# Two normalisations of a step answered by one GpSimd addition and one power over eight columns

## The reference, cut to what matters

```python
def _layer_norm(t, gamma, beta):
    mu = jnp.mean(t, axis=-1, keepdims=True)
    var = jnp.mean(jnp.square(t - mu), axis=-1, keepdims=True)
    return (t - mu) * jax.lax.rsqrt(var + LN_EPS) * gamma + beta
...
moe_out = jnp.einsum('bseh,bse->bsh', expert_out, sparse)
return _layer_norm(x + moe_out, gamma, beta)
```

## Time and profile before

| | |
|---|---|
| median of three executions | 2806.18 us (2802.29 to 2806.91) |
| the profiled execution, its own time | 2819.77 us |
| span of its profile | 2817.9 us |
| busy: PE, DVE, ACT, POOL | 84%, 70%, 54%, 35% of the span |
| the phase that is changed | from about 1868 to 2325 us of the span |

### The profile page before, as it was taken

How to read it: one execution, slowest core, us unless ns; L and a number is a source line. 1 busy time by engine, 2 the same in 40 slices (tenths; PEclk the granted TensorE clock), 3 DMA queues, 4 the chain that set the end, 5 groups by cost and what they waited for, 6 DMA issues and landing times. The chain is left out here.

```text
span 2817.9 us, 45185 instructions
## 1 busy us (share of the span) xinstructions
PE 2376.4 (84%) x14046; PEld 1704.3 (60%) x14047; DVE 1983.6 (70%) x5404; ACT 1514.0 (54%) x2636; POOL 999.0 (35%) x1024
## 2 busy tenths in 40 slices
PE   8999999999996999999964999926788885666665
PEld 4444444444444788888854999925677774444443
DVE  6777777777745788888853444447687877888886
ACT  2444444444442667676743665636565651777776
POOL 1100100100000355555552444468776720344343
PEclk9999999999997999999976999967687786677676
DMA  2000000000002011111116777731111100000000
GB/s 56 0 18 13 0 18 13 0 9 1 0 1 86 27 45 48 47 47 47 47 58 204 256 255 256 253 98 51 46 46 41 47 13 22 20 24 22 25 25 25
DMA packets 69334, 162.68 MB, mean 58 GB/s; under 512 B 13009, under 2 KB 32662, under 8 KB 68894
## 3 DMA queue, kind: packets, MB, share of 16 engines
q1 hardware_dynamic: 39618, 94.16, 10.2%
q0 software_dynamic: 21504, 44.99, 5.5%
q10 hardware_dynamic: 8064, 21.68, 2.5%
HBM read 63.87 MB, written 63.88 MB: 45 GB/s over the span
## 5 line engine op out<-in xcount | busy, mean ns | idle before, releaser
L418 DVE TENSOR_REDUCE pmax<-ppre 112x1 f32<-112x512 f32 x656 | 424.0, 686 | 161.6 <-PE ppre L260 161.5
L211 ACT ACTIVATE prob<-pscore 128x896 f32<-128x896 f32 x336 | 308.1, 917 | 421.9 <-PE pscore L293 421.9
L307 PE MATMUL pout<-prob,xkey 128*64 128x448 f32 x1344 | 327.5, 566 | 0.4 <-ACT prob L211 0.4
L718 POOL DMA_INDIRECT rows_in<-xr,idx x224 | 233.9, 1044 | 237.2 <-DVE idx L1189 180.2
L260 PE MATMUL ppre<-xh,yh 49*112 49x512 f32 x656 | 291.1, 446 | 7.8 <-DVE pmax L418 4.2
L260 PEld LDWEIGHTS ppre<-xh,yh 49*112 49x112 f32 x656 | 112.6, 172 | 239.1 <-issue 104.2
L1631 POOL DMA_INDIRECT yg<-rows_out,place x224 | 234.7, 1048 | 62.4 <-issue 62.1
L193 POOL CAST yh<-ynext 113x448 fp32r<-113x448 f32 x28 | 17.3, 616 | 666.4 <-DVE pmax L418 638.4
L293 PE MATMUL pscore<-yh,xh 49*128 49x448 f32 x700 | 241.1, 422 | 0.4 <-DVE yh L438 0.4
L2146 POOL TENSOR_TENSOR yg<-y,gout 112x512 f32<-112x512 f32 x112 | 141.2, 1271 | 265.5 <-DVE y L2379 265.5
L1481 POOL TENSOR_TENSOR zl<-z,zh 128x448 fp32r<-128x448 f32 x126 | 144.7, 1149 | 219.2 <-ACT zh L1447 209.8
(11 more groups left out here) (367 smaller groups left out, 6464.5 us busy)
## 6 DMA issues: line engine op xcount, KB each, us to landing
wd<-down SPq DMA_DIRECT2D x63, 512.0 KB, 3.0
xb<-rows_in SPq DMA_DIRECT2D x63, 448.0 KB, 3.6
rows_out<-yb ACTq DMA_DIRECT2D x63, 336.0 KB, 3.2
out<-ho SPq DMA_DIRECT2D x28, 336.0 KB, 2.8
rows_in<-zero SPq DMA_DIRECT2D x15, 448.0 KB, 5.3
rows_in<-xr,idx POOLq DMA_INDIRECT x224, 2.5
yg<-rows_out,place POOLq DMA_INDIRECT x224
xkey<-in_xkey SPq DMA_DIRECT2D x4, 800.0 KB, 6.8
```

The lines of the kernel that those rows point to most:

```text
L211: nc.scalar.activation(prob[j % 3][:, :, :], pscore[j % 2][:, :, 0:CH], ACT.Exp).then_inc(exped, 1)
L307: mm = pe.matmul(pout[i * LO:(i + 1) * LO, 0:CH], xkey[b % 2][:, 2 * j + i, :], prob[j % 3][:, i, :], start=(j == 0), stop=(i == 1 and j = ...
L418: nc.vector.reduce_max(pmax[:, q, 2 * block + half:2 * block + half + 1], bank(u, depth), AX.X).then_inc(pre_max, 1)
L718: nc.gpsimd.indirect_dma_start(rows_in, bass.IndirectOffsetOnAxis(ap=idx[r % G3][:, 2 * q + k:2 * q + k + 1], axis=0), xr[r % G3][:, q, :] ...
```

## The change

The statistics of both normalisations go into one tile `agg3[T, 2, TPC, 2]`, and `veps3`, `rst3`, `eps5_3` and `mhalf_3` get the same extra index of 2. GpSimd's `factor(s+3)` and `factor4(s+2)` become one `factors(s+3)`. It waits for the aggregates of both, then does one addition and one power over [112, 8]. It stands where `factor` stood, ahead of the last two gathers of the step. `offset` reads column 0 of it, `offset4` column 1, and `offset4(g)` now waits for the same count as `offset(g+1)`.

```diff
-            def factor(g):
-                pool.wait_ge(S["agg_out"], g + 1)
-                nc.gpsimd.tensor_tensor(veps[:], agg[:, :, 1], eps5[:], ALU.add).then_inc(S["veps_out"], 1)
+            def factors(g):
+                cols = slice(0 if here(g) else 1, 2 if here(g - 1) else 1)
+                if here(g):
+                    pool.wait_ge(S["agg_out"], g + 1)
+                if here(g - 1):
+                    pool.wait_ge(S["agg4_out"], g)
+                nc.gpsimd.tensor_tensor(veps[:, cols, :], agg[:, cols, :, 1], eps5[:, cols, :],
+                                        ALU.add).then_inc(S["veps_out"], 1)
                 pool.wait_ge(S["veps_out"], g + 1)
                 if g >= 1:
                     pool.wait_ge(S["nrm_out"], g)
-                nc.gpsimd.tensor_tensor(rst[:], veps[:], mhalf[:], ALU.pow).then_inc(S["rst_out"], 1)
-
-            def factor4(g):
-
-                pool.wait_ge(S["agg4_out"], g + 1)
-                nc.gpsimd.tensor_tensor(veps4[:], agg4[:, :, 1], eps5[:], ALU.add).then_inc(S["veps4_out"], 1)
-                pool.wait_ge(S["veps4_out"], g + 1)
-                if g >= 1:
-                    pool.wait_ge(S["xn_ready"], g)
-                nc.gpsimd.tensor_tensor(rst4[:], veps4[:], mhalf[:], ALU.pow).then_inc(S["rst4_out"], 1)
+                if g >= 2:
+                    pool.wait_ge(S["xn_ready"], g - 1)
+                nc.gpsimd.tensor_tensor(rst[:, cols, :], veps[:, cols, :], mhalf[:, cols, :],
+                                        ALU.pow).then_inc(S["rst_out"], 1)

             for s in range(-LEAD, NC):
                 if here(s + 4):
                     gather_rows(s + 4, (0, 1, 2))
-                if here(s + 3):
-                    factor(s + 3)
+                if here(s + 3) or here(s + 2):
+                    factors(s + 3)
                 if here(s + 4):
                     gather_rows(s + 4, (3,))
-                if here(s + 2):
-                    factor4(s + 2)
...
             def offset4(g):
-                dve.wait_ge(S["rst4_out"], g + 1)
-                nc.vector.scalar_tensor_tensor(off4[:], agg4[:, :, 0], -1.0, rst4[:], ALU.mult,
+                dve.wait_ge(S["rst_out"], g + 2)
+                nc.vector.scalar_tensor_tensor(off4[:], agg[:, 1, :, 0], -1.0, rst[:, 1, :], ALU.mult,
                                                ALU.mult).then_inc(S["off4_out"], 1)
```

More of the change, by code:

```diff
@@ L1553, in linear_attention_phase @@
         bet = sb("bet3", [T, D])
-        eps5 = sb("eps5_3", [T, TPC])
-        mhalf = sb("mhalf_3", [T, TPC])
+        eps5 = sb("eps5_3", [T, 2, TPC])
+        mhalf = sb("mhalf_3", [T, 2, TPC])
         yg = [sb(f"yg3_{i}", [T, TPC, 2, D]) for i in range(2)]
@@ L1559, in linear_attention_phase @@
         bn = sb("bn3", [T, TPC, 6])
-        agg = sb("agg3", [T, TPC, 2])
-        veps = sb("veps3", [T, TPC])
-        rst = sb("rst3", [T, TPC])
+        agg = sb("agg3", [T, 2, TPC, 2])
+        veps = sb("veps3", [T, 2, TPC])
+        rst = sb("rst3", [T, 2, TPC])
         off = sb("off3", [T, TPC])
         bn4 = sb("bn4", [T, TPC, 6])
-        agg4 = sb("agg4", [T, TPC, 2])
-        veps4 = sb("veps4", [T, TPC])
-        rst4 = sb("rst4", [T, TPC])
         off4 = sb("off4", [T, TPC])
@@ L1595, in linear_attention_phase @@
         names = ("e_in", "w_in", "w_ready", "xa_out", "half_out", "acc_out", "stat_out", "agg_out", "veps_out",
-                 "rst_out", "off_out", "nrm_out", "dvec3", "hm_out", "stat4_out", "agg4_out", "veps4_out", "rst4_out",
+                 "rst_out", "off_out", "nrm_out", "dvec3", "hm_out", "stat4_out", "agg4_out",
                  "off4_out", "xn_ready", "xtr_mm", "xH_out", "xL_out", "xT_out", "qk_mm", "b_sum", "a_sum",
@@ L1822, in rows_normed @@
                     ac = nc.scalar.activation(yf[:, q, :], acc[g % 3][:, q, :], ACT.Identity, bias=off[:, q:q + 1],
-                                              scale=rst[:, q:q + 1])
+                                              scale=rst[:, 0, q:q + 1])
                 ac.then_inc(S["nrm_out"], 1)
@@ L1833, in normalise @@
                         ac = nc.scalar.activation(xn[g % 2][:, q, cols], h[:, t, src], ACT.Identity,
-                                                  bias=off4[:, q:q + 1], scale=rst4[:, q:q + 1])
+                                                  bias=off4[:, q:q + 1], scale=rst[:, 1, q:q + 1])
                 ac.then_inc(S["xn_ready"], 1)
@@ L1897, in add_experts @@
                 for q in range(TPC):
-                    ag = nc.vector.bn_aggr(agg[:, q, :], bn[:, q, :])
+                    ag = nc.vector.bn_aggr(agg[:, 0, q, :], bn[:, q, :])
                 ag.then_inc(S["agg_out"], 1)
@@ L1903, in offset @@
                 dve.wait_ge(S["rst_out"], g + 1)
-                nc.vector.scalar_tensor_tensor(off[:], agg[:, :, 0], -1.0, rst[:], ALU.mult,
+                nc.vector.scalar_tensor_tensor(off[:], agg[:, 0, :, 0], -1.0, rst[:, 0, :], ALU.mult,
                                                ALU.mult).then_inc(S["off_out"], 1)
@@ L1921, in add_moe @@
                 for q in range(TPC):
-                    ag = nc.vector.bn_aggr(agg4[:, q, :], bn4[:, q, :])
+                    ag = nc.vector.bn_aggr(agg[:, 1, q, :], bn4[:, q, :])
                 ag.then_inc(S["agg4_out"], 1)
             def offset4(g):
-                dve.wait_ge(S["rst4_out"], g + 1)
-                nc.vector.scalar_tensor_tensor(off4[:], agg4[:, :, 0], -1.0, rst4[:], ALU.mult,
+                dve.wait_ge(S["rst_out"], g + 2)
+                nc.vector.scalar_tensor_tensor(off4[:], agg[:, 1, :, 0], -1.0, rst[:, 1, :], ALU.mult,
                                                ALU.mult).then_inc(S["off4_out"], 1)
```

## The result

The changed kernel takes 2839.09 us (median of four executions, 2833.55 to 2841.30) beside 2804.23 us before: a ratio of 1.0118, interval 1.0103 to 1.0134, 35 us slower. The forecast was +24 us, 2830, with a range from 2809 to 2837: the first comparison lies above the range.

What follows compares the result with a forecast made beforehand. GpSimd and DVE were taken to set the pace together in steady steps. Late gathers gave 9.23 us, 17 x 0.83 made it 23.3, plus 2 less 0.4 to 2.7 at the turns: +24 us, 2830 us, range 2809 to 2837.

Steps and rivals of the forecast that it cites:

- T: End of the second normalisation's aggregates in a step, the last thing the second power needs; distances run from it to DVE's products.
- the loop closes: Late products delay the statistics queued behind them on DVE, hence the next T: a step of 14.26 us plus x.
- the second stretch: Four steady distances from T = 2056.37 to 2102.45: 19.92 us before, 22.16 forecast, +2.24 us and 4x.
- x: Extra time of a GpSimd power over eight columns against four: between 0 and 0.83 us, taken as 0.83.
- The first stretch: Eight steady distances from T = 1891.81 to the products at 1994.22: 41.37 us before, 44.32 forecast, +2.95 us and 8x.
- The three steps into a turn: Steps where gram_turned lies between T and products: the power's wait goes, -2.9 us in all; with x, -0.4 to -2.7.
- the turns: Six other distances at the turns: no change from gathers, but with x the second offset is late, +2 us in all.
- The phase: Time from the first T to the last, where the forecast's steps lie; 406.9 us in the first profile of before.
- rival 1: A power is paid for the instruction, not its columns: x near 0, +6 us, 2812; chance 0.25.
- rival 2: Faster: the late gathers land in time for DVE's products, -20 us, 2786; chance 0.08.
- rival 3: Gathers land later than forecast or the turns stretch, half a microsecond more a step: +33 us, 2839; chance 0.10.
- The rule on the landing: Gather data land 2.2 us from the issue's start, not 2.64: each distance 0.44 shorter, sum +16 us at x = 0.83.

Runs made afterwards that it cites:

- the place alone: The kernel before with the last two gathers of a step moved behind the second power, both additions and powers kept apart: 2817.7 against 2808.3 us, ratio 1.0033.
- the trial instructions: The changed kernel plus unused GpSimd additions and powers of 1 to 32 columns behind its last factors; whole time not used, power over 8 columns measured 1.64 us.
- the next two: The changed kernel, unchanged, compared again with the kernel before: 2833.5 against 2808.3 us, ratio 1.0090, then 2831.5 against 2805.3 us, ratio 1.0093.
- one late: The changed kernel with one gather behind the joined power instead of two: 2817.0 against 2805.3 us, ratio 1.0038.

## Why the prediction was right or wrong

**The sign and the mechanism were right**, step by step. GpSimd stands at its wait when T comes; the last two gathers start behind the power; the products wait for their landing in 21 steps (I gave 17 to 20); the loop closes through the statistics. Both halves are shown by doing them alone: the place alone gives distances of 5.5 us (forecast 5.54), the width in the trial instructions gives the rest, and undoing the place turns the sign. Luck has little part in it, but some: see the second stretch below.

**The terms.** The power ends at T + 2.10 (forecast 1.41 + 0.83 = 2.24), the issues take 2.44 (2.43), the landing 1.73 (1.70): a distance of 6.27 where I had 6.37. x is 0.69, of which 0.62 is the power, 1.67 against 1.05; the remaining 0.07 is the start of the addition at T + 0.15, which in the earlier trace rows was at T + 0.08. I had taken everything above an addition as work for columns; 0.2 us of it is the instruction's. The stretches came to 50.0, 26.8 and 25.3 us against forecasts of 51.0, 25.5 and 25.5, from the 41.4, 19.9 and 19.5 of before. The first stretch is 1 us under the forecast and the second, with two distances of 7.1 and 7.0 us that the chain doesn't give, 1 us over; that they cancel is chance. The three steps into a turn gained 0.2 (forecast -2.7 to -0.4). For the turns I had +2. Between the first two profiles they gave back 2.2 us (distances 57.8 to 56.2, the way from the products to T 59.7 to 59.1), but the second profile of before has 53.8 for the distances: the turns differ by 4 us between two profiles of one kernel, and my +2 is neither shown nor refuted. The phase in all: +22.0 us between the first two profiles, and +23 on the mean of three profiles after and two before (428.2 against 405.3). The sum was right to a few us.

**The rule on a GpSimd operation's price fell, for a power.** The section 3.1 of "GPSIMD Engine Reference" in the Trainium skill, with 2.6 cycles for an element, would by an estimate have made four more columns some 9 ns. They cost 630. For additions the trace agrees: 0.20 us at 8 columns and 0.25 at 32, 2 ns each. **The rule on the landing** (the Trainium skill, "DMA: Bandwidth & Descriptors", the anatomy of one DMA on GpSimd's path, from which the forecast estimated 2.2 us from the issue) was short here: 2.67 us from the start of the last issue to the products.

**What failed is the range, by a term that the sum leaves out.** The step of the prediction is that differences inside one profiled execution are "then laid on the median", and from it "The whole range, 2809 to 2837, takes in most of rival 1 and leaves out rival 2 and the upper half of rival 3". The range was built from the bounds of the mechanism and laid on a median of three executions. The difference of everything outside the phase was put at nothing, without a reason. In the first comparison it was 11 to 13 us: 35 us of time against 22 to 24 of phase. In the next two it was 1 to 5. What follows the last T is code that the change doesn't touch, and in the profiles it took 507.5 to 521.1 us. The feed-forward in it, to the end of the span, in the first profiles of before and of after, each from 110 us behind the last T (start:end, length, busy us of PE, PEld, DVE, ACT, POOL, clock, DMA):

```profile
2408.70:2817.90 409.20, 261.93 (x1500) 175.56 (x1497) 344.36 (x885) 292.91 (x507) 160.88 (x133) 0.71 0.09 24
```

```profile
2432.20:2831.20 399.00, 245.26 (x1500) 167.37 (x1498) 345.13 (x885) 293.45 (x507) 160.71 (x133) 0.77 0.09 25
```

The same instructions on DVE, ACT and POOL; 17 us more of PE's busy time at a granted clock of 0.71 than at 0.77, and 10 us more of span. Over the ten other profiles, three of them of these same two kernels, it goes the same way: 397.5 us at 0.77 and 411.1 at 0.70 are the ends, with one exception (407.8 at 0.76, where the trial instructions still run on GpSimd in the stretch ahead). So code that no version changes spans 14 us. Repeated profiles of one kernel differ less (409.2 and 407.4 before; 399.0, 401.0 and 401.1 after), so profiles alone don't show that this span belongs to no kernel. But times of one kernel do spread, and I had the sign of it in hand: the profiled execution lay 13.6 us above the median. Executions of one kernel in one comparison spread over 3 to 24 us. Four against four, as in the first comparison, then give 35 with an interval of 29 to 38 us by its own scatter, and the next two 25 and 26. The later medians, 2833.5 and 2831.5, lie in the range.

**The time goes with the granted clock of the execution**, which is on record, as a mean over the whole program, beside nearly every time. The executions of before are those of the later comparisons and the first profiled one, put together:

| mean granted clock | the kernel before, us | the changed kernel, us |
|---|---|---|
| 0.882, 0.883 | 2818.4, 2819.8 | none |
| 0.884, 0.885 | none | 2837.1, 2837.7, 2841.1, 2841.3 |
| 0.891 | six, 2808.1 to 2812.2, mean 2809.6 | 2832.9, 2833.0, 2834.1 |
| 0.896 | six, 2802.1 to 2806.9, mean 2804.3 | 2828.5, 2829.7 |

At 0.891 and at 0.896 the change costs 24 and 25 us, which is the forecast, and the phase has 22 to 24. Three of the four executions of the changed kernel in the first comparison were at 0.884 or 0.885, and one of the eleven in the next two: its median of 2839 goes with that. For the four executions of before in that comparison no clock is on record. What sets the clock of an execution no run here shows; the changed kernel's mean is 0.003 and 0.004 under that of before in the second and third comparison (0.8915 and 0.8940, 0.8912 and 0.8953), so a part of the lower clock may come from the change itself.

**What stays open.** I didn't see a profile of an execution of 2839 us, nor one of before at 2804, so that the 10 us between the comparisons lie in the feed-forward is argued and not shown; that they go with the clock is. And three of the comparisons of kernels whose products wait for gathers had more in time than in phase: 9 against 5 us (gathers late, factors apart), 12 against 5 (one late), 35 against 24 (the first comparison), though the other two comparisons of the changed kernel had 25 and 26 against 24 and 21. A cost of some us behind the phase isn't excluded. Rival 3 named late landing and the turns; neither happened.

**A version that beats both** is the joined one with all eight gathers first: 0.9970 (0.9957 to 0.9982).

## What to carry to other kernels

Joining two small operations makes them wait for the later of their inputs, and whatever is queued behind them on the engine waits too. Before joining, list what stands behind the first of the two, and move it ahead of the join if it has no need of it: here the same join loses 25 us with two gathers behind it (35 in one comparison) and gains 10 with none. And before giving a range for a difference of about one per cent, look at how much the times of one unchanged kernel differ, and compare executions at the same granted clock.

## What the runs showed of the hardware

- A power on GpSimd over 112 partitions takes 0.56, 0.70, 1.01, 1.64, 2.91 and 5.44 us for 1, 2, 4, 8, 16 and 32 columns; an addition 0.19 to 0.25.
- Most of GpSimd's issues of an indirect DMA take 0.93 to 1.00 us, with 0.3 between two. Beside DVE's products of the gathered rows many take about 1.15. Those of the phase of before that run beside DVE's product and additions over 768 columns with both operands in SBUF take up to 1.8, and 2.7 in three cases.
- The power over four columns takes 1.65 us instead of 1.04 when it begins while such an addition runs. That made one of the two powers of before look dearer than the other (1428 against 1044 ns in the earlier trace rows). With the second factor first, where the same power runs at another time, it takes 1.01 to 1.04.
- One unchanged kernel takes 2799 to 2820 us, and its time goes with the mean granted clock of the execution: 2804.3 us on the mean at 0.896, 2809.6 at 0.891.
